# The first batch's mixture of experts, sorted by expert through DRAM

## The reference, cut to what matters

```python
h = _layernorm(x) * (1 + ca) + sa
x = x + ga * attention(h)                  # causal, with a distance mask
h = _layernorm(x) * (1 + cb) + sb
topk_idx, tw = _route(h, router_w, bias)   # 4 of 16 experts, tw sums to 2.5
combine = (one_hot(topk_idx, 16) * tw[..., None]).sum(1)
g = einsum('td,edf->etf', h, gate_w)
u = einsum('td,edf->etf', h, up_w)
y = einsum('etf,efd->etd', silu(g) * u, down_w)
sh = silu(h @ sh_gate_w) * (h @ sh_up_w) @ sh_down_w
x = x + gb * (einsum('etd,te->td', y, combine) + sh)
```

## Time and profile before

| | us |
|---|---|
| median of 2 runs | 629.06 (628.48 to 629.63) |
| the profiled execution | 626.02 |
| its span, first to last instruction | 624.3 |
| TensorE busy | 556.8 (89%) |
| VectorE busy | 490.7 (79%) |
| ScalarE busy | 363.7 (58%) |
| GpSimd busy | 353.4 (57%) |

### The profile page before, as it was taken

One profiled execution on the slowest core, in us unless ns is written; L12 is line 12 of the kernel. 1 busy time (PEld: TensorE's weight loads), 2 busy tenths in 40 slices (PEclk: granted clock), 3 DMA queues, 4 the chain that ended last, 5 costly groups with the idle time before them and its releaser, 6 DMA issues. The chain is left out here.

```text
span 624.3 us, 10923 instructions
## 1 busy us (share of the span) xinstructions
PE 556.8 (89%) x3508; PEld 334.7 (54%) x3508; DVE 490.7 (79%) x1428; ACT 363.7 (58%) x729; POOL 353.4 (57%) x339
## 2 busy tenths in 40 slices
PE   6898778978767998989989999899798999999996
PEld 5655445556534543545545555555455565656664
DVE  6869999987867896459667667558986999989886
ACT  5267657885436334546866776674447555545552
POOL 7678659351035518497876696453215555555553
PEclk9989999989879999989999999999999999999998
DMA  8500100000042212312012121121100000000000
GB/s 220 147 2 2 38 1 1 2 1 2 5 120 68 74 64 68 84 53 85 17 56 94 39 69 34 51 85 53 34 1 17 3 13 7 2 19 1 18 2 18
DMA packets 23425, 26.02 MB, mean 42 GB/s; under 512 B 2676, under 2 KB 13960, under 8 KB 23368
## 3 DMA queue, kind: packets, MB, share of 16 engines
q1 hardware_dynamic: 22928, 24.80, 13.6%
q10 hardware_dynamic: 440, 0.53, 0.3%
HBM read 23.09 MB, written 2.23 MB: 41 GB/s over the span
## 5 line engine op out<-in xcount | busy, mean ns | idle before, releaser
L621 POOL TENSOR_TENSOR sw<-hid,gp 128x512 f32<-128x512 f32 x64 | 81.4, 1271 | 80.4 <-DVE hid L1690 75.2
L635 POOL TENSOR_TENSOR gp<-stage,gp 128x512 f16<-128x512 f32 x72 | 83.8, 1164 | 65.5 <-ACT gp L847 65.5
L1690 DVE SCALAR_TENSOR_TENSOR hid<-stage,bank 128x512 f32<-128x512 f32 x72 | 49.3, 685 | 56.4 <-ACT stage L830 55.8
L830 ACT ACTIVATE stage<-bank 128x512 f32<-128x512 f32 x144 | 84.6, 589 | 15.1 <-PE bank L881 14.7
L571 POOL TENSOR_TENSOR row<-row,dx 128x512 f32<-128x512 f32 (+3 forms) x48 | 55.7, 1160 | 51.1 <-ACT dx L686 50.5
L782 ACT COPY ptr<-bank 128x512 f32<-128x512 f32 (+2 forms) x80 | 41.4, 518 | 70.4 <-PE bank L1082 69.3
L847 ACT CAST gp<-stage 128x512 f16<-128x512 f32 x72 | 44.4, 617 | 64.6 <-DVE stage L1753 64.6
L1100 PE MATMUL bank<-v,ptr 128*128 128x128 f32 x544 | 76.3, 281 | 4.6 <-DVE x L1508 4.6
L1201 PE MATMUL bank<-stage,wd 128*128 128x512 f32 x144 | 75.3, 605 | 5.0 <-DVE x L1697 5.0
L1100 PEld LDWEIGHTS bank<-v,ptr 128*128 128x128 f32 x544 | 69.6, 197 | 7.2 <-issue 5.8
L1736 DVE SCALAR_TENSOR_TENSOR x<-bank,comb,x 128x128 f32<-128x128 f32 x256 | 71.5, 342 | 0.1
(11 more groups left out here) (251 smaller groups left out, 1270.3 us busy)
## 6 DMA issues: line engine op xcount, KB each, us to landing
gp<-shares SPq DMA_DIRECT2D x64, 256.0 KB, 3.2
out_x<-x SPq DMA_DIRECT2D x8, 256.0 KB, 2.3
x<-in_L_attn_hidden_states SPq DMA_DIRECT2D x4, 256.0 KB, 5.3
stage<-in_L_ffn_gate_w SPq DMA_DIRECT2D x1, 576.0 KB, 5.0
stage<-in_L_ffn_up_w SPq DMA_DIRECT2D x1, 576.0 KB, 4.2
stage<-in_L_ffn_gate_w SPq DMA_DIRECT2D x1, 448.0 KB, 5.5
stage<-in_L_ffn_up_w SPq DMA_DIRECT2D x1, 448.0 KB, 3.4
row<-in_L_wmod ACTq DMA_DIRECT2D x1, 384.0 KB
```

The source lines that it names most:

```text
L621: pool.tensor_tensor(sw[:, s % 2, :], hid[:, s % 2, :], wb[:, n % HELD_WEIGHTS, :], ALU.mult)\
L635: pool.tensor_tensor(gp[:, n % HELD, 1, :], act_g[:, s % 2, :], gp[:, n % HELD, 0, :], ALU.subtract)\
L830: act.activation(sg[:, s % 2, :], gate_bank(s)[:, :], func, scale=half_of / (H_UP * W_UP))\
```

## The change

Only the first batch's mixture is computed in another way; the second batch's mixture keeps its 72 steps and its arithmetic.

- Each token's row of `h` is turned back to token-major form (`turn_rows`, `copy_rows`, into `hrow`). From the routing's hits VectorE and TensorE count, for each expert, the tokens ahead of a token (`cumulate`, three products with a triangle and with ones), and `slots` makes for each token four places in a table of 80 tiles of 128 rows, where each tile belongs to one expert. It also makes the list of the tiles' experts, `tile_expert`.
- GpSimd writes the rows to their places in `sorted_rows` in DRAM with 64 indirect DMAs of 128 rows of 512 bytes, 32 at step 15 of the inputs and 32 at step 24. The table has been filled before with finite rows by five DMAs of 1 MB.
- The 80 tiles are worked on as 20 quads of four tiles, at steps 52 to 71, beside the last 20 slots of the second batch's attention. A quad is loaded (`load_sorted`), turned (`turn_quad`), split, goes through gate and up (24 products of 128x128 in f16), tanh and two VectorE operations, and through four fp32 down products of 128x128; ScalarE copies the result, and SyncE stores it to `result_rows`.
- The weights of a tile's expert are fetched by SyncE: it loads the expert's number into a register and issues a DMA of 128 KB within SBUF for gate and up and one of 64 KB from `down_rows` in DRAM for down. There is room for two quads (`GU_HELD`, `DOWN_HELD`). The down weights are multiplied by the gate vector ahead (`gate_downs`) and stored to `down_rows`.
- The two shared experts are computed for all tokens in 8 units at steps 8 to 22, and added to `x`.
- The routed results come back beside the second batch's mixture: GpSimd gathers the four rows of each token with 64 indirect DMAs, four after every fourth step (`fetch_results`), and VectorE adds them with their weights, 64 operations (`add_results`).
- `weigh`, `shares`, `hidden`, `output` and the steps of the first batch go. GpSimd subtracts the measure for the second batch from chunk 10 on, and VectorE makes the first ten.

```diff
-POOL_FROM = CHUNKS_BEFORE[14]
+POOL_FROM = (CHUNKS_BEFORE[14], CHUNKS_BEFORE[7])
 LOGITS_AT = max(SPLIT_AT) + 1
 ROUTE_AT = {SLOTS - 4 - ROUTE_PARTS + n: n for n in range(ROUTE_PARTS)}
-COMB_AT = {SLOTS - CH + 1 + n: n for n in range(CH - 1)}
-HELD_WEIGHTS = 3
+CUMULATE_AT = max(ROUTE_AT) + 1
+
+
+TILES = (N * TOP + E * (P - 1)) // P
+QUADS = -(-TILES // PER)
+TILES = QUADS * PER
+SHARED = NS * CH
+UNITS = SHARED + QUADS
+SHARED_FROM = 8
+QUADS_FROM = PIECES + SLOTS - QUADS
+GATES_AT = {SHARED_FROM + 2 * u: u for u in range(SHARED)} | {QUADS_FROM + j: SHARED + j for j in range(QUADS)}
+DOWNS_AT = {t + 1: u for t, u in GATES_AT.items() if u >= SHARED or u % NS}
+TURNS_AT = {t - 1: u - SHARED for t, u in GATES_AT.items() if u >= SHARED}
+UNITS_END = max(DOWNS_AT) + 1
+GATED_AT = max(WEIGHTS_AT) + 1
+GU_HELD = 2
+DOWN_HELD = 2
+SCATTER_FIRST = 15
...
-        def run(first, inputs, attention, step, late, finish=None):
+        def run(first, inputs, attention, group, step, late, finish=None):
 
 
 
@@ -303,19 +345,21 @@
                 if finish:
                     finish(0, n)
                 attention(0, n)
-            for s in range(NB * STEPS + 3):
-                b, t = divmod(s, STEPS)
-                if finish and b + 1 < NB and 0 <= t - PIECES < SLOTS:
-                    finish(b + 1, t - PIECES)
-                step(s)
-                if b < NB and t < (LATE_STEPS if b + 1 < NB else LATE_END):
-                    late(b, t)
-                if b + 1 < NB:
-                    n = t - PIECES
-                    if n < 0:
-                        inputs(b + 1, t)
-                    if 0 <= n < SLOTS:
-                        attention(b + 1, n)
+            for t in range(UNITS_END):
+                n = t - PIECES
+                if finish and 0 <= n < SLOTS:
+                    finish(1, n)
+                group(t)
+                if t < LATE_STEPS:
+                    late(0, t)
+                if n < 0:
+                    inputs(1, t)
+                elif n < SLOTS:
+                    attention(1, n)
+            for d in range(STEPS + 3):
+                step(d)
+                if d < LATE_END:
+                    late(1, d)
 
         def ring(b, which, n):
 
@@ -325,30 +369,31 @@
...
+            def fetch_weights(j):
+
+                for k in range(PER):
+                    m = j * PER + k
+                    e = sp.value_load(tile_expert[m:m + 1, 0:1], min_val=0, max_val=E - 1)
+                    if j >= GU_HELD:
+
+                        sp.wait_ge(up_made, SHARED + j - GU_HELD + 1)
+                    at = m % (GU_HELD * PER)
+                    sp.dma_start(gu_held[:, at:at + 1, :, :], wgu[:, bass.ds(e, 1), :, :]).then_inc(gu_loaded[j % GU_HELD], 16)
+                    if j >= DOWN_HELD:
+
+                        sp.wait_ge(down_made, SHARED + j - DOWN_HELD + 1)
+                    at = m % (DOWN_HELD * PER)
+                    sp.dma_start(down_held[:, at:at + 1, :], down_rows[bass.ds(e, 1), :, :].rearrange("e f d -> f e d"))\
+                      .then_inc(down_loaded[j % DOWN_HELD], 16)
+
+            def load_sorted(j):
+
+                if j >= 2:
+                    sp.wait_ge(quad_turned, j - 1)
+                sp.dma_start(sorted_in[:, j % 2, :, :], quad_rows(sorted_rows, j)).then_inc(sorted_loaded[j % 2], 16)
+
+            def store_quad(j):
+
+                sp.wait_ge(result_copied, j + 1)
+                sp.dma_start(quad_rows(result_rows, j), result_out[:, j % 2, :, :]).then_inc(result_stored[j % 2], 16)
 
             def store_result(f):
...
+            sp.wait_ge(gated_stored, 32)
+            sp.wait_ge(tiles_ready, 1)
+            fetch_weights(0)
+            sp.wait_ge(scattered, 16 * TOP * BLK)
+            load_sorted(0)
+            load_sorted(1)
+            fetch_weights(1)
+            for j in range(QUADS):
+                if j + 2 < QUADS:
+                    load_sorted(j + 2)
+                    fetch_weights(j + 2)
+                store_quad(j)
             for c in range(CH):
...
+            def scatter(blocks):
+
+                for i in blocks:
+                    for k in range(TOP):
+                        pool.indirect_dma_start(sorted_rows, bass.IndirectOffsetOnAxis(slot[:, i, k:k + 1], 0),
+                                                hrow[:, i, :], None).then_inc(scattered, 16)
+
+            def fetch_results(i):
+
+                if i >= PER:
+                    pool.wait_ge(result_added, i - PER + 1)
+                for k in range(TOP):
+                    pool.indirect_dma_start(fetched[:, i % PER, k, :], None, result_rows,
+                                            bass.IndirectOffsetOnAxis(slot[:, i, k:k + 1], 0))\
+                        .then_inc(result_fetched[i % PER], 16)
+
...
+                if k == SCATTER_FIRST:
+                    pool.wait_ge(slots_ready, 1)
+                    pool.wait_ge(rows_filled, 16 * (TILES // BLK))
+                    for n in range(2):
+                        pool.wait_ge(rows_copied[n], 2)
+                    scatter(range(0, BLK // 2))
                 if k == PIECES - 1:
-                    for m in range(2):
-                        measure(b, m)
...
+                if d % 4 == 2 and d // 4 < BLK:
+                    if d // 4 == 0:
+                        for n in range(2):
+                            pool.wait_ge(result_stored[n], 16 * QUADS // 2)
+                    fetch_results(d // 4)
...
+            def turn_quad(j):
+
+                pe.wait_ge(sorted_loaded[j % 2], 16 * (j // 2 + 1))
+                if j:
+                    pe.wait_ge(quad_split, j)
+                for k in range(PER):
+                    last = pe.transpose(bank[5][:, k * P:(k + 1) * P], sorted_in[:, j % 2, k, :], ident[:, :])
+                last.then_inc(quad_turned, 1)
+
+            def shared_gate_up(u):
...
+            def quad_gate_up(j):
+
+                u, at = SHARED + j, j % GU_HELD * PER
+                pe.wait_ge(quad_split, j + 1)
+                pe.wait_ge(gu_loaded[j % GU_HELD], 16 * PER * (j // GU_HELD + 1))
+                pe.wait_ge(hidden_ready, u)
+
+                def products(dst, which):
+                    for k in range(PER):
+                        lot = slice(k * P, (k + 1) * P)
+                        last = pair(dst[:, lot], [gu_held[:, at + k, which + h, :] for h in range(2)],
+                                    [quad_input(j)[:, h, lot] for h in range(2)])
+                    return last
+
+                products(bank[3], 0).then_inc(gate_made, 1)
+                pe.wait_ge(act_ready, u)
+                products(bank[4], 2).then_inc(up_made, 1)
+
+            def unit_down(u):
...
+                j = u - SHARED
+                pe.wait_ge(down_loaded[j % DOWN_HELD], 16 * PER * (j // DOWN_HELD + 1))
+                if j:
+                    pe.wait_ge(result_copied, j)
+                else:
+                    pe.wait_ge(shared_added, CH)
+                for k in range(PER):
+                    lot = slice(k * P, (k + 1) * P)
+                    last = mm(bank[6][:, lot], act_g[:, u % 2, lot], down_held[:, j % DOWN_HELD * PER + k, :],
+                              start=True, stop=True)
+                last.then_inc(down_made, 1)
+
...
+            def slots():
+
+                dve.wait_ge(rank_made, 1)
+                dve.wait_ge(measure_ready, pooled(0, NCH - 1))
+                wide = equal16[:, :, :]
+                step(dve.tensor_scalar(need[:, :], bank[7][:, BLK * E:(BLK + 1) * E], 1.0 / P, None, ALU.mult)); settle()
+                step(dve.tensor_tensor(wide, need[:, :].unsqueeze(2).broadcast_to([P, E, E]),
+                                       iota[:, :].unsqueeze(1).broadcast_to([P, E, E]), ALU.is_gt)); settle()
+                step(dve.tensor_reduce(need[:, :], wide, X, ALU.add)); settle()
+                step(dve.tensor_tensor(wide, need[:, :].unsqueeze(1).broadcast_to([P, E, E]), tri16[:, :, :], ALU.mult))
+                settle()
+                step(dve.tensor_reduce(starts[:, :], wide, X, ALU.add)); settle()
+                rank = bank[7][:, 0:BLK * E].rearrange("p (i e) -> p i e", e=E)
+                step(dve.scalar_tensor_tensor(out=place, in0=rank, scalar=1.0,
...
+            def add_results(i):
+
+                dve.wait_ge(result_fetched[i % PER], 16 * TOP * (i // PER + 1))
+                dve.wait_ge(shared_added, i // PER + 1)
+                dve.wait_ge(chosen_ready, 1)
+                own = x[:, i, :]
+                for k in range(TOP):
+                    last = dve.scalar_tensor_tensor(out=own, in0=fetched[:, i % PER, k, :], scalar=chosen[:, i, k:k + 1],
+                                                    in1=own, op0=ALU.mult, op1=ALU.add)
+                    if k + 1 < TOP:
+                        step(last); settle()
+                last.then_inc(result_added, 1)
+                if i % PER == PER - 1:
```

(2 more changed lines are left out.)

562 lines of the change are left out of this document (316 added, 246 removed).

## The result

The changed kernel took 843.51 us (842.82 to 844.20) against 629.06: a ratio of 1.341, 95% interval 1.334 to 1.348. Run again later, unaltered, it took 823.12 us (821.53 to 826.62), a ratio of 1.311, interval 1.305 to 1.317. Both are far slower than before. Slower was forecast too, but 725 us, with a range of 622 to 830: the first result lies above that range, the second just inside it. The accounting is made against the second, "the kernel run again".

A forecast was written before the change was run, and what follows sets the result against it. TensorE's queue looked nearly full, but GpSimd's and SyncE's queues were expected to set the pace: quads end at 541, plus 175 for the last mixture and 3 of store, span 719; plus 1.7 and 3, 724, said as 725; range 622 to 830.

The forecast's parts named there:

- so I take 70 us: Second batch's inputs, from 170 us: 70 us, between bounds of 58 and 94, so its attention starts at 240.
- I leave that to the range (up to 2.2 us more per quad): Quads: a quiet TensorE may fall to the lower clock; not in the sum, only in the range.
- The last mixture, 175 us: Last 75 steps: gathers on GpSimd's queue make 147 us into 175, +28; VectorE's 153 lies below.
- TensorE's 82 us of relief: Whole kernel: mixture steps removed from TensorE, less shared units and quads added, relieve it of about 82 us.
- the three charges: Scatters and gathers at 1.16 us each on GpSimd, register loads at 0.9 us each on SyncE.
- nothing gained: Second batch's inputs: upper bound of 94 us, the stretch as long as before.
- The stall at slot 10: Second batch's attention: slot 10 waits for GpSimd behind 64 scatters, 302 instead of 271.5, a stall of 30 us.
- The period of the quads: Down product to down product: issues, loads, landing, products and semaphore steps make 10.1 us, bounds 7.3 and 12.5.
- Cheap descriptors: Rival: indirect DMAs cost at most 0.47 us, loads nearly nothing; 625 us, no change (0.10), or faster (0.10).
- 494 + 18 p: Cheap-descriptor rival's whole time, p being the quads' period; 625 us at 7.3, 584 at TensorE's own 5 us.
- Heavier scatters: Rival: scatters of 2 us each delay slot 10, the quads and the last stretch; 831 us, chance 0.15.
- Loads of 1.7 us: Rival: register loads as long as a small DMA, period 12.5 us, 768 us in all, chance 0.15.

The follow-up runs named there:

- `warm`: The changed kernel with ten unused f16 TensorE products of 512 columns in front of each quad's wait for its weights: 808.96 us.

## Why the prediction came out as it did

**Which steps failed.** The direction and its reasons held, and the sizes did not: 725 us was forecast, +96 against the kernel before, and +194 and +214 came. The span of the kernel run again is 101 us above the forecast span, from three terms that were all too small:

- The inputs, "so I take 70 us": the first scatter came 26 us late. With what follows from it, the first down product was 41 us late.
- The quads, "I leave that to the range (up to 2.2 us more per quad)": TensorE's fall to its lower level was put at nothing in the sum. It was there in most quads, 22 us in all.
- The last mixture, 175 us, the larger of GpSimd's and VectorE's work: the two don't overlap like that. They lie on one chain by turns, and VectorE's adds were priced by an operation of another kind: 38 us.

The late semaphores added 20 us more in the first run; no term held them, and without them the time would have been just inside the range.

**The direction.** GpSimd's and SyncE's queues, not TensorE's 82 us of relief, set the time. Each of the three charges was found where it was said to be, and taking each away gave back 32 to 69 us (gathers 31.6, scatters 38.5, register loads 68.6).

**"I take 70 us" for the inputs** (26 us short at the first scatter). The estimate came from VectorE's work, 58 us and gaps. VectorE is busy 36 of the 62 us from 173 to 235; the chain runs through all four engines by turns. The trace before had the answer, and I did not read it: GpSimd's root and deviation, which the scatters stand behind, are in it at

```profile
188.68 2.90 POOL L519 TENSOR_TENSOR rs<-ve,minus_half 128x16 f32<-128x16 f32 x1 [1.00 <-DVE ve L1241]
212.75 2.90 POOL L514 TENSOR_TENSOR runit<-nrm,minus_half 128x16 f32<-128x16 f32 x1 [1.03 <-DVE nrm L1346]
225.45 0.57 POOL L514 TENSOR_TENSOR sdv<-var,half 128x1 f32<-128x1 f32 x1 [0.74 <-DVE var L1371]
```

and in the changed kernel, run again, at

```profile
183.69 2.97 POOL L591 TENSOR_TENSOR rs<-ve,minus_half 128x16 f32<-128x16 f32 x1 [8.64 <-DVE ve L1415]
220.68 2.90 POOL L586 TENSOR_TENSOR runit<-nrm,minus_half 128x16 f32<-128x16 f32 x1 [33.64 <-DVE nrm L1520]
235.22 0.57 POOL L586 TENSOR_TENSOR sdv<-var,half 128x1 f32<-128x1 f32 x1 [11.64 <-DVE var L1545]
```

The chain did not become shorter with the mixture gone; its last link came 10 us later. Up to the root `rs` it did gain 5 us, although the first batch's attention ended some 3 us late, where the forecast had 0. From there to `runit` it took 37 us in place of 24. TensorE's fp32 projections in this part take 2.05 to 2.08 us a pair in part where they took 1.02 to 1.13: a part of the reason, read and not tested. The operations that the change adds on VectorE there, the slots and the shared units, are a rival that no run parts from it. My upper bound, "nothing gained" (94 us), was the right value: 170 + 94 = 264, and slot 0 came at 265.5.

**The stall at slot 10** was right in place and kind: forecast 30 us, 34.0 measured, at 338 in place of 302. A stall of 13.2 us at slot 4, for the base of group 0, was not forecast; it adds nothing to the second, as GpSimd's queue sets the end of both. Of the 36 us, 26 are the late start and 7 are 64 x (1.27 - 1.16). From slot 10 to 27 the forecast was 47, and 56.1 were measured (56.5 without scatters, so it isn't they); these 9 us have no explanation here. The Trainium skill's figure of about 1 us for a software DMA (DMA: Bandwidth & Descriptors, "Latency and other measured facts") is the time to its first byte, which it puts down to what GpSimd does to emit it. The trace agrees in size, with 0.96 us for which one holds GpSimd; the sum needs the distance to the next, and that is 1.27 us.

**The period of the quads**: 10.1 forecast, 11.4 measured (11.77 in the quad shown). Issues and loads: 5.52 forecast, 5.47 measured; landing: 2.1 against 1.59; products and steps: 2.45 against 4.71. The mechanism was right, and the first two terms were near. The failed step is "I leave that to the range (up to 2.2 us more per quad)": the lowest granted clock of the kernel before was 0.96, and it was taken over for a stretch in which the same sum has TensorE work 5 of 10 us. The granted clock there was 0.77, and the products of the quad shown were at 1.2 GHz. That term, 2.26 us more, is the whole difference; the shorter landing takes 0.5 back. The `warm` run, which raised the clock to 0.93, shows it as a cause. For the register load 0.9 was taken and 0.72 to 0.81 measured. The Trainium skill has a floor of about 600 ns for it (the same section), and the trace agrees: all three lie above.

**The last mixture**: 175 forecast (178 with the store), 216 measured. Three errors add up. The gathers were taken at 1.16 us and cost 1.27: 7 us. The adds were taken at 342 ns, an operation with one operand in PSUM; the new ones have both in SBUF and take 761 ns in the mean: 20 us. And I took the larger of GpSimd's 175 and VectorE's 153, where both lie on one chain by turns: the adds alone already made 150 into 169.6, and the gathers came on top with 27. That is the remaining 11, a difference and not a measurement of its own.

**The rivals.** Cheap descriptors (625, no change) is out: even without scatters, gathers and register loads the kernel takes 674. Its sum, 494 + 18 p with p = 7.3, had slot 27 at 319 where it came at 352.5, p was 8.2, and the last stretch 169 in place of 157. Heavier scatters (831) come near the first run, and for a wrong reason: a scatter takes 1.27 us, not 2. Loads of 1.7 us is out, with 0.72 to 0.81 measured. The late semaphores were in none of the cases. So the second result's place inside the range is in part luck: the range's upper end came from scatters of 2 us, and was filled by other terms.
